# Second layer: probabilities turned by VectorE in 32x32 squares, value product in 32x64 tiles, fp32 scores

## The reference

```
h = Wqkv[half] @ z + Winj[half] @ u          # 128 -> 3 * 1024, other weights for each half of the positions
q, k, v = split(h)
score = (q + r_w_bias) . k / 8               # 256 x 256 for each head and batch entry
prob  = softmax(score)
attn  = prob @ v                             # 64 x 256 for each head
x = Wo @ attn + bo + z
out = (x - mean) / sqrt(var + eps)           # over the 128 features
```

## Time and profile before

| | |
|---|---|
| median of 3 runs | 1515.6 us (1515.39 to 1516.03) |
| the profiled execution | 1517.32 us, its span 1515.6 us |
| PE / PEld busy | 1330.7 us (88%) / 999.7 us (66%) |
| DVE / ACT / POOL busy | 1003.3 us (66%) / 888.4 us (59%) / 649.5 us (43%) |
| second layer | from about 638 us to 1400 us of the span |

### The profile page before, as it was taken

How to read it: one execution, slowest core, us unless ns; L and a number is a source line. 1 busy time by engine, 2 the same in 40 slices (tenths; PEclk the granted TensorE clock), 3 DMA queues, 4 the chain that set the end, 5 groups by cost and what they waited for, 6 DMA issues and landing times. The chain is left out here.

```text
span 1515.6 us, 29849 instructions
## 1 busy us (share of the span) xinstructions
PE 1330.7 (88%) x9586; PEld 999.7 (66%) x9586; DVE 1003.3 (66%) x2031; ACT 888.4 (59%) x3038; POOL 649.5 (43%) x615
## 2 busy tenths in 40 slices
PE   4678898898989776589999999999999999996897
PEld 2444565565656454478888888888888888884464
DVE  3477777777777844376666666676676667664354
ACT  2476767677776734365656656555565555553443
POOL 3487676766666632023334333333333333342000
PEclk9899999999999998789999999999999999998899
DMA  4030000000000000010000000000000000000110
GB/s 158 1 140 18 5 15 3 14 10 7 10 7 3 11 0 1 28 43 2 8 1 9 0 0 7 0 7 0 0 7 0 7 0 0 2 1 1 51 42 28
DMA packets 18509, 24.54 MB, mean 16 GB/s; under 512 B 1360, under 2 KB 16912, under 8 KB 18064
## 3 DMA queue, kind: packets, MB, share of 16 engines
q1 hardware_dynamic: 18448, 23.77, 4.8%
HBM read 21.67 MB, written 2.10 MB: 16 GB/s over the span
## 5 line engine op out<-in xcount | busy, mean ns | idle before, releaser
L953 POOL TENSOR_TENSOR prob<-prob,l_z_inv 128x512 f32<-128x512 f32 x256 | 261.2, 1042 | 457.2 <-DVE l_z_inv L1194 457.2
L1113 ACT ACTIVATE prob<-psum,l_neg_max 128x256 f32<-128x256 f32 x512 | 236.0, 473 | 240.5 <-DVE l_neg_max L1188 240.5
L618 ACT ACTIVATE ring_e<-ring_e,neg_max 128x128 f32<-128x128 f32 x512 | 199.4, 395 | 98.8 <-DVE neg_max L758 98.3
L409 POOL TENSOR_TENSOR ring_e<-ring_e,z_inv 128x512 f32<-128x512 f32 x128 | 174.2, 1361 | 139.5 <-DVE z_inv L753 139.5
L1188 DVE TENSOR_REDUCE l_neg_max<-psum 128x2 f32<-128x512 f32 x256 | 163.9, 682 | 10.6 <-PE psum L1007 10.6
L1035 PE MATMUL psum<-pT,vs 128*64 128x256 f32 x1024 | 138.8, 391 | 6.7 <-DVE aTl L1204 6.7
L1019 PEld LDWEIGHTS psum<-ident,prob 128*128 128x128 f32 x1024 | 109.8, 141 | 49.0 <-issue 45.4
L1019 PE MATMUL psum<-ident,prob 128*128 128x128 f32 x1024 | 139.9, 280 | 0.0
L521 PE MATMUL psum<-ident,ring_e 128*128 128x128 f32 x512 | 85.7, 292 | 50.7 <-ACT ring_t L625 49.7
L1199 DVE COPY pT<-psum 128x512 f32<-128x512 f32 x128 | 88.1, 689 | 51.0 <-PE psum L1019 51.0
L521 PEld LDWEIGHTS psum<-ident,ring_e 128*128 128x128 f32 x512 | 55.8, 144 | 81.5 <-issue 77.3
(11 more groups left out here) (196 smaller groups left out, 3510.3 us busy)
## 6 DMA issues: line engine op xcount, KB each, us to landing
wz_raw<-wz_in SPq DMA_DIRECT2D x2, 1536.0 KB, 10.4
x_in<-x SPq DMA_DIRECT2D x8, 256.0 KB, 2.7
cT<-ctxT SPq DMA_DIRECT2D x8, 256.0 KB, 2.7
w<-w_in SPq DMA_DIRECT2D x2, 1024.0 KB, 11.5
l_ub<-ctx_in SPq DMA_DIRECT2D x8, 256.0 KB, 2.8
cg<-ctx_in SPq DMA_DIRECT2D x4, 512.0 KB, 3.5
out<-fin SPq DMA_DIRECT2D x4, 512.0 KB, 2.8
wi_raw<-wi_in SPq DMA_DIRECT2D x1, 1536.0 KB, 15.2
```

The costliest lines, as they stand in the source:

```text
L409: pool.tensor_tensor(p, p, z_inv[:, n % RE, :].unsqueeze(2).broadcast_to([P, QUAD, P]), ALU.mult)\
L618: last = nc.scalar.activation(e, e, ACT.Exp, bias=neg_max[:, n % RE, h:h + 1], accum_out=z_sum[:, n % RE, h:h + 1])
L953: pool.tensor_tensor(e, e, z_inv[:, t % RE, h, :].unsqueeze(2).broadcast_to([P, 2, D]), ALU.mult)\
L1113: last = nc.scalar.activation(prob[:, t % RE, h, qt * D:(qt + 1) * D], score_bank[h][:, qt * D:(qt + 1) * D], ACT.Exp, bias=neg_max[:, t % ...
```

## The change

The turning leaves PE. `nc.vector.transpose` on DVE turns every 32x32 square of a 128x512 tile in place, so a key lies in its square's partition, not in its own row of a whole transposed tile: partition quarter a (32 partitions) then holds the probabilities of the queries of quarter a, against key s of each of the 8 key blocks. For the product, each quarter needs the values of all keys in its own 32 partitions. So ACT copies a values' tile to `vs`, SP writes it to DRAM (`l1_values`, 256 KB a tile, 8 tiles a round), and four transfers of 128 KB a step read it back, one to each quarter, into a ring `vr` of four buffers. `times_v` becomes 64 fp32 matmuls of 32 rows, 64 weight columns and 64 moving columns: 8 key blocks x 4 quarters x 2 heads, into four banks.

The scores become four fp32 matmuls for a step; q and k are kept in fp32, written by ACT alone. The output product is made two pairs at a time, six matmuls in the fills `o0` to `o3` (steps 6, 10, 14, and 2 of the next round), in the two banks of `work`, and DVE adds the four shares up in `part`. `FILLS` is written anew: no turning, no `wo` bank, fills moved by one step at some places.

```diff
-    L_T, L_V, L_W = 1, 2, 4
+    L_T, L_V = 1, 2
+    SQ = 32
+    QUARTERS, KEYS = P // SQ, D // SQ
+    RV = 4
+    values = nc.dram_tensor("l1_values", (H1 // 4 * NB, D, 4 * HD1), F32).ap()
...
-        FILLS = [("q1", "k1"), ("v0b1", "q2"), ("k2",), ("v1b0", "q3"), ("k3", "v1b1"), ("q4", "mean"), ("k4",),
-                 ("v2b0", "q5", "var"), ("k5",), ("v2b1", "q6"), ("k6", "v3b0"), ("q7", "k7"), ("v3b1", "inv0"),
-                 ("inv1",), ("q0+", "k0+"), ("v0b0+",)]
+        FILLS = [("q1", "k1"), ("v0b1", "q2"), ("o3", "k2"), ("v1b0", "q3"), ("k3", "v1b1"), ("q4", "mean"),
+                 ("k4", "o0"), ("v2b0", "q5", "var"), ("k5",), ("v2b1", "q6"), ("o1", "k6"), ("v3b0", "q7"),
+                 ("k7", "v3b1", "inv0"), ("inv1",), ("o2", "q0+"), ("k0+", "v0b0+")]
...
+            def save_values(i, g, b):
+                tile = g * NB + b
+                sp.wait_ge(*work.out(f"v{g}b{b}", i))
+                for t in (4 * g + b, 4 * g + NB + b):
+                    sp.wait_ge(*spread_in[t % RV].at(i - 1, t // RV))
+                sp.dma_start(values[tile].rearrange("(c p) f -> p c f", p=P), vs[:, :, :])\
+                    .then_inc(values_out.sem, 16)
+
+            def spread_values(i, t):
+                pair, b = divmod(t, NB)
+                tile = pair // 2 * NB + b
+                sp.wait_ge(*values_out.at(i, tile))
+                sp.wait_ge(*pv_done.at(i, t - RV))
+                at = pair % 2 * 2 * HD1
+                src = values[tile][:, at:at + 2 * HD1].rearrange("(c s) f -> s c f", s=SQ)
+                for a in range(QUARTERS):
+                    sp.dma_start(vr[a * SQ:(a + 1) * SQ, t % RV, :, :], src).then_inc(spread_in[t % RV].sem, 16)
...
                 for qt in range(2):
-                    for qp, kp in ((0, 0), (0, 1), (1, 0)):
+                    for h in range(2):
+                        rows = slice(h * HD1, (h + 1) * HD1)
+                        last = mm(score_bank[h][:, qt * D:(qt + 1) * D], q[rows, pair % 2, qt, b, :],
+                                  k[rows, pair % 2, :, b, :], start=True, stop=True)
...
+            def times_v(i, t):
+                for h in range(2):
+                    pe.wait_ge(*turned.at(i, 2 * t + h))
+                pe.wait_ge(*spread_in[t % RV].at(i, t // RV))
+                pe.wait_ge(*aT_lo.at(i, t - 1))
+                for c in range(KEYS):
+                    for a in range(QUARTERS):
+                        rows = slice(a * SQ, (a + 1) * SQ)
                         for h in range(2):
...
+                            last = mm(pv_banks[a][h * HD1:(h + 1) * HD1, :],
+                                      vr[rows, t % RV, c, h * HD1:(h + 1) * HD1],
+                                      pT[rows, h, :].rearrange("p (t c r) -> p t c r", t=2, r=SQ)[:, :, c, :],
+                                      start=c == 0, stop=c == KEYS - 1)
...
+            def times_wo(i, name, m):
+                slots = (0, 1) if m % 2 == 0 else (2, 3)
                 pe.wait_ge(*work.free(name, i))
+                pe.wait_ge(*aT_lo.at(i - 1 if m == 3 else i, 4 * m + 3))
+                for slot in slots:
+                    for wp, ap in ((0, 0), (0, 1), (1, 0)):
...
-            def copy_turned(i, t):
-                act.wait_ge(*turned.at(i, 2 * t))
-                act.wait_ge(*pv_done.at(i, t - 1))
-                nc.scalar.copy(pT[:, 0, :], turn_bank[0]).then_inc(copied[0].sem, 1)
...
+                if name[0] == "v":
+                    g, b = int(name[1]), int(name[3])
+                    act.wait_ge(*values_out.at(i, g * NB + b - 1))
+                    nc.scalar.copy(tile_of(name), work.psum(name)).then_inc(work.reads(name), 1)
...
+            def turn(i, t, h):
+                dve.wait_ge(*probs_done.at(i, 2 * t + h))
                 dve.wait_ge(*pv_done.at(i, t - 1))
-                nc.vector.tensor_copy(pT[:, 1, :], turn_bank[1]).then_inc(copied[1].sem, 1)
+                nc.vector.transpose(pT[:, h, :], prob[:, t % RE, h, :]).then_inc(turned.sem, 1)
...
+            def add_product(i, name, m):
+                dve.wait_ge(*work.full(name, i))
```

More of the change, by code:

```diff
@@ L888, in layer1 @@
             "scores_done", "max_done", "exp_done", "z_inv_done", "probs_done", "turned"))
-        copied = [event(f"pT{h}_copied", STEPS) for h in range(2)]
+        values_out = event("values_out", H1 // 4 * NB, 16)
+        spread_in = [event(f"values_spread{j}", STEPS // RV, 16 * QUARTERS) for j in range(RV)]
         pv_done = event("pv_done", STEPS)
@@ L1013, in turn @@
[L1013 to L1036, removed]
-                last.then_inc(pv_done.sem, 1)
@@ L1039, in times_wo @@
[L1039 to L1043, removed]
-                    last = mm(wo_bank, wo[wp][:, pair, :], aT[ap][:, pair % 2, :, :].rearrange("p b d -> p (b d)"),
-                              start=(pair, wp, ap) == (0, 0, 0), stop=(pair, wp, ap) == (PAIRS - 1, 1, 0))
-                last.then_inc(wo_done.sem, 1)
@@ L1051, in mean @@
+            def mean(i, name, product):
+                pe.wait_ge(*work.free(name, i))
+                pe.wait_ge(*work.out(product, i))
                 mm(work.psum(name), mean_w[:, :], y[:, :, :].rearrange("p b d -> p (b d)"),
@@ L1083, in body @@
                             project(r, name)
+                        elif name == "o3" and first:
+                            pe.wait_ge(*work.free(name, i))
+                            mm(work.psum(name)[:, 0:1], mean_w[:, :], mean_w[:, 0:1], start=True, stop=True)\
+                                .then_inc(work.fills(name), 1)
+                        elif name[0] == "o":
+                            if first and name == "o0":
+                                pe.wait_ge(wo_lo_made, 1)
+                            times_wo(r, name, int(name[1]))
                         elif name == "mean":
-                            mean(r, name)
+                            mean(r, name, "o3")
                         elif name == "var":
@@ L1288, in body @@
                         if is_made(name):
-                            rest_work(r, name)
+                            continue
+                        if name == "o3" and first:
+                            dve.wait_ge(*work.full(name, i))
+                            nc.vector.memset(y[:, :, :], 0.0).then_inc(work.reads(name), 1)
+                        elif name[0] == "o":
+                            add_product(r, name, int(name[1]))
                         elif name == "mean":
```

167 lines of the change are left out of this document (70 added, 97 removed).

## The result

The changed kernel is slower: 1592.39 us in the median of four runs (1584.19 to 1602.45), against 1515.82 (1515.39 to 1516.38) for the kernel before on the same chip, a ratio of 1.051 with an interval of 1.044 to 1.058. I had forecast 1465 us, a gain, in a range of 1440 to 1640. The profiled execution took 1602.45 us, its span is 1600.7.

A forecast was written before the change was run, and what follows sets the result against it. PE was taken to set the pace: the second layer's steps summed to 84.4 us, 85.0 with late values, against 91.27; eight rounds save 50, so 1517.3 becomes 1467, median 1465. Range 1440 to 1640.

The forecast's parts named there:

- the first rival: Issue bounds the value product's tile records: 1527 us at 12.5 ns a record, 1724 at 25 ns; chance 0.26.
- Value product: PE's product in 64 tile matmuls, 128 records a step: 1.25 us, bounds 1.06 to 3.4.
- step 8: Step of the second layer's 16-step round, counted from 0: set by the loop over maxima and exponentials, 3.87 us.
- Scores: PE's fp32 scores in each step, 8 records in place of 12: 1.05 us, bounds 0.90 to 1.9.
- Turn: DVE's turning of one 128x512 tile, two a step: 0.69 us, upper bound 1.2.
- Step 7: Step of the second layer's round, counted from 0: 6.93 us less 0.47, so 6.46.
- step 13: Step of the second layer's round: set by the loop over maxima and exponentials, 3.72 plus 0.15, so 3.87 us.
- step 14: Step of the second layer's round: its maxima wait for DVE's splitting of the next round's inputs, 6.2 us.
- Product and projection: Steps 2, 6 and 10 of a round, with an output product and a projection: 5.32 us each.
- Late values: Two value tiles through DRAM, wanted in steps 3 and 11: 0.6 us a round; as a rival 1509 us, chance 0.11.
- The layer's end: End of the second layer, left alone in the sum: less than 1 us either way.
- The clock: PE's granted clock falling if its new gaps lengthen: named second among the ways to be wrong, without size or chance.

The follow-up runs named there:

- the pair in the kernel before: The kernel before the change, with two rounds written out in PE's loop body, turning three times instead of six: 1521.25 us, ratio 1.0025.
- v3: The changed kernel without tiles: turned squares moved through DRAM, value product of four fp32 matmuls four steps behind the scores: 1447.84 us, 0.954 of the kernel before.

## Why the prediction was wrong

**The step that failed** is the first rival's own sentence, "A loop so large may be fetched again each time; no row prices that". I counted the records (780 to about 2500), had the 33 packets in view, and then gave it no price, only a share in a chance. It was to be bounded by what it does: fetched again or not. It is, in every round, and costs some 13.4 of the 14.3 us: 7.5 in stalls at a few places, and 5.9 that go with the clock falling behind them. It is shown by the stops themselves, which end behind packets and, without the loop, stand a multiple of 256 instructions apart, by the runs with one block and with four (no fetch and 77.0; 14 fetches and 84.9, where its clean steps make 79.6), by the pair in the kernel before, and by v3, which has all of the change but the tiles and holds 81.3. That 1592 lies inside my range is luck: the range reached so far up for tiles that follow each other at 12.5 ns or more, and they follow at 10.8. The direction, for which I gave 0.66 to faster, was wrong. The Trainium skill (Runtime: NRT & Kernel Launch, Instruction fetch mechanics) says that PE's memory holds 2048 instructions, refilled in blocks of 256, and that crossing a block is "mostly hidden". The lists that stay (1554 and 1708) and the one that doesn't (2002) don't contradict the size, if instructions that leave no record are added to the last. "Mostly hidden" holds for the pair in the kernel before and not here, where 22 packets a round cost some 13.4 us. That a taken branch breaks the prefetch, as it says, is seen at 1056.36.

**Value product.** 1.25 taken, 1.52 measured, between my bounds of 1.06 and 3.4 and short of the 1.70 from which the first rival decides. It follows from about 10.8 ns a record, where I had taken some 8 (1.04 us for 128). The Trainium skill's 25 ns between matmuls (TensorE: Matmul & The Clock Gate, part 1) doesn't hold between such tiles: 128 records in 1.5 us. Fourteen steps at 0.27 are 3.8 us a round, and the sum of 84.4 becomes 88.2, the clean sum: rate wrong by a fifth, mechanism right. Step by step it is spread otherwise: 0.3 in each of the seven steps of two projections, 0.34 in step 8, nothing in steps 7 and 14.

**What held.** Scores 1.06 (1.05, my forecast in brackets). Turn 0.69 (0.69). DVE 59.2 us a round (59). Step 7 6.44 (6.46; since PE is busy throughout and its product is 0.27 longer, something else in it is shorter than I took), step 13 3.88 (3.87), step 14 6.2 where clean (6.2, in the version without a loop). Product and projection 5.59, which is 5.32 and 0.27. Step 8 takes 4.21, not 3.87: with the longer product the loop over the exponentials isn't what bounds it.

**Late values.** 0.6 us a round forecast, 0.9 seen; hidden more by PE's own delays than by my slack of 0.7, as the run with one block shows: there PE waits 2.8 us in a round for them, in steps 3 and 11.

**The layer's end** was taken as less than 1 us. From the start of the last step of the second layer to the end of the span the kernel before has 138.5 us, the changed one 148.7, v3 148.2. The new order of work at the end isn't the reason: the run with four key blocks has the same order, and 138.6 (with one block 139.4). In the changed kernel it is the step that failed once more. Each of the last two products stops in its middle,

```profile
1461.86 1.03 PE L1061 MATMUL psum<-pT,vr 32*64 32x64 f32 x42 [1.90 <-issue]
1468.32 1.02 PE L1061 MATMUL psum<-pT,vr 32*64 32x64 f32 x43 [1.98 <-issue]
```

and the granted clock is at its lower level from 1458.30 to 1495.84, 37.5 us, where the kernel before has 20.5 us of it. In v3, which has no packet near, PE waits 2.7 us for the squares and stops twice, 4.7 us, for nothing that the profile shows; its 10 us stay unexplained. With the rounds it closes for the changed kernel: the first 127 steps take 719.0 us before and 795.5 after, 76.5 more; the end 10.2 more, the start 1.6 less; 85.1, and the profiled times differ by 85.1.

**The clock** I had named as the second danger, for gaps that lengthen. That was right in kind. I gave it no case of its own.

**Open.** What decides when a block is asked for: in the version without the loop PE went on for some 1.3 us into a product before it stopped for 3.7 us (975.93 to 980.89), at other places than with the loop, for the same total. And why halves of the product didn't help. No run separates a late request from a slow one.

## What to carry to other kernels

Count the instructions of an engine's loop body, not only the time of its records: if it is longer than what is seen to stay (here 1708 stay, 2002 don't), fetching it in every round needs a price of its own, above all where many short instructions stand together. Work taken from an engine by cutting its matmuls small comes back as such a list; here a gain of the forecast size was to be had by moving the data into the shape of a few large matmuls. A transfer is priced with its issue, 0.45 to 0.60 us each on the queue that sends it.

## What the runs showed that I had not expected

- Tile matmuls of 32x64 with 64 columns follow each other every 10.6 to 11.3 ns a record, two records an fp32 matmul, weight loads included.
- A list of 5138 instructions a round, fetched in 16 KB packets, costs the same with and without the jump back: 1592 and 1594 us. Without it every stop of over 0.4 us marked issue stands a multiple of 256 instructions behind the one before, to within one.
- A turn of a short loop on PE costs some 0.26 us (3.5 us for 132 records in 8 turns; 0.14 with 4 turns), and the clock has a mean of 0.88 in the round with 8.
- A transfer of 32 KB inside the core's memory holds SP for 0.60 us, one of 128 KB from DRAM for 0.45.
- The granted clock stays at 1.00 beside transfers of 210 GB/s, with DMA busy 0.74 of the time.
